# A hybrid state-space / attention / mixture-of-experts layer: copies of Q and K through outside memory, and two projections at other places of a shared bank's order

## What is computed

```python
# three sub-layers; x is (8, 512, 128) float32, every step adds to the residual stream
def _L0_attn_a_ref(x, W_in, Kx, Kz, W_xproj, W_dt, b_dt, A_log, D, W_out):     # state-space layer
    h = jnp.einsum('bld,ed->ble', x, W_in)
    xb, zb = jnp.split(h, 2, axis=-1)
    xb = _dwconv_silu(xb, Kx)
    zb = _dwconv_silu(zb, Kz)
    proj = jnp.einsum('blc,oc->blo', xb, W_xproj)
    dt_raw, b_raw, c_raw = proj[..., :8], proj[..., 8:16], proj[..., 16:]
    delta = jnp.clip(jax.nn.softplus(jnp.einsum('blr,cr->blc', dt_raw, W_dt) + b_dt), 0.0001, 1.0)
    b_term, c_term = jnp.tanh(b_raw), jnp.tanh(c_raw)
    a = jax.nn.softplus(A_log) + 0.0001
    decay = jnp.clip(jnp.exp(-delta[..., None] * a), 0.0001, 1.0)
    drive = (1.0 - decay) * (b_term[:, :, None, :] * xb[..., None])
    # scan over time: state = decay*state + drive;  y = sum(state*c) + D*xb
    return jnp.einsum('bld,ed->ble', jnp.concatenate([y, zb], axis=-1), W_out)

def _L0_attn_b_ref(hidden_states, Wq, bq, Wk, bk, Wv, bv, Wo, bo):             # attention, 16 heads of 8
    q, k, v = proj(hidden_states, Wq, bq) * scaling, proj(..., Wk, bk), proj(..., Wv, bv)
    scores = jnp.einsum('bhsd,bhtd->bhst', q, k) + chunk_attention_mask(S)     # chunks of 10, 25 to the left
    out = jnp.einsum('bhst,bhtd->bhsd', jax.nn.softmax(scores, axis=-1), v)
    return jnp.einsum('bse,fe->bsf', out, Wo) + bo

def _L0_ffn_ref(x, w_router, w_gating, w_gate, w_up, w_down):                  # 8 experts, all of them
    g = jnp.einsum('bsh,ehf->ebsf', x, w_gate)
    u = jnp.einsum('bsh,ehf->ebsf', x, w_up)
    expert_out = jnp.einsum('ebsf,efh->ebsh', jax.nn.silu(g) * u, w_down)
    return jnp.einsum('ebsh,bse->bsh', expert_out, cw)                         # cw: routing weights

x = x + _L0_attn_a_ref(_layernorm(x), ...)
x = x + _L0_ffn_ref(_layernorm(x), ...)
x = x + _L0_attn_b_ref(_layernorm(x), ...)
x = x + _L0_ffn_ref(_layernorm(x), ...)
```

## Time and profile before

| what | us |
|---|---|
| three runs: lowest, median, highest | 1697.87, 1698.93, 1699.07 |
| the profiled execution, its own time | 1692.36 |
| its span (first to last instruction) | 1690.5 |
| outside the span | 1.86 |

### The profile page before, as it was taken

How to read it: one execution, slowest core, us unless ns; L and a number is a source line. 1 busy time by engine, 2 the same in 40 slices (tenths; PEclk the granted TensorE clock), 3 DMA queues, 4 the chain that set the end, 5 groups by cost and what they waited for, 6 DMA issues and landing times. The chain is left out here.

```text
span 1690.5 us, 31436 instructions
## 1 busy us (share of the span) xinstructions
PE 1560.0 (92%) x12484; PEld 1305.2 (77%) x12484; DVE 1025.8 (61%) x2316; ACT 949.1 (56%) x1302; POOL 410.8 (24%) x403
## 2 busy tenths in 40 slices
PE   5389978999999899998999999989999999999998
PEld 2278866888778787787878778777788888888887
DVE  5556656765766567666665576556755675476543
ACT  5273737753686456836666486356743665276421
POOL 5332331422213222124211241113411221022000
PEclk9999989999999999999999999999999999999999
DMA  5010110002000200010001200021001000100000
GB/s 180 13 38 26 60 55 10 34 10 57 2 22 31 58 12 2 29 53 34 8 1 36 77 3 8 1 74 41 1 1 51 7 1 2 51 2 8 1 7 7
DMA packets 39426, 47.11 MB, mean 28 GB/s; under 512 B 5120, under 2 KB 21504, under 8 KB 39280
## 3 DMA queue, kind: packets, MB, share of 16 engines
q1 hardware_dynamic: 39280, 45.10, 8.7%
HBM read 25.97 MB, written 2.33 MB: 17 GB/s over the span
## 5 line engine op out<-in xcount | busy, mean ns | idle before, releaser
L948 ACT ACTIVATE h<-pg 128x512 f32<-128x512 f32 x512 | 304.5, 598 | 609.5 <-PE pg L261 607.0
L892 PE MATMUL pd<-w_down,h 128*128 128x128 f32 x4096 | 544.3, 282 | 0.6 <-DVE x L974 0.6
L892 PEld LDWEIGHTS pd<-w_down,h 128*128 128x128 f32 x4096 | 511.3, 195 | 31.5 <-issue 9.0
L994 DVE TENSOR_TENSOR h<-h,pu 128x512 f32<-128x512 f32 x512 | 347.2, 680 | 187.4 <-PE pu L261 185.9
L799 POOL TENSOR_TENSOR att_arena<-att_arena 100x500 f32<-100x500 f32 (+2 forms) x192 | 172.9, 900 | 613.5 <-DVE att_arena L741 605.8
L259 PE MATMUL pg<-ffn_x_hi,w_gate_hi 128*128 128x512 f32 x512 | 247.7, 484 | 0.0
L259 PE MATMUL pu<-ffn_x_hi,w_up_hi 128*128 128x512 f32 x512 | 205.7, 402 | 9.5 <-DVE h L994 9.5
L260 PE MATMUL pg<-ffn_x_lo,w_gate_hi 128*128 128x512 f32 x512 | 205.6, 402 | 0.0
L261 PE MATMUL pg<-ffn_x_hi,w_gate_lo 128*128 128x512 f32 x512 | 205.1, 401 | 0.0
L260 PE MATMUL pu<-ffn_x_lo,w_up_hi 128*128 128x512 f32 x512 | 205.0, 400 | 0.0
L261 PE MATMUL pu<-ffn_x_hi,w_up_lo 128*128 128x512 f32 x512 | 204.7, 400 | 0.0
(11 more groups left out here) (170 smaller groups left out, 1778.5 us busy)
## 6 DMA issues: line engine op xcount, KB each, us to landing
arena<-bc_spread SPq DMA_DIRECT2D x56, 256.0 KB
q<-qk_parts SPq DMA_DIRECT2D x128, 64.0 KB, 2.1
k<-qk_parts SPq DMA_DIRECT2D x128, 64.0 KB, 2.1
arena<-in_x SPq DMA_DIRECT2D x8, 256.0 KB, 2.8
x<-in_x SPq DMA_DIRECT2D x8, 256.0 KB, 3.3
h<-in_w_gate SPq DMA_DIRECT2D x8, 256.0 KB, 6.5
h<-in_w_up SPq DMA_DIRECT2D x8, 256.0 KB, 2.8
w_down<-in_w_down SPq DMA_DIRECT2D x8, 256.0 KB, 4.3
```

Source lines behind the costliest of these rows:

```text
L892: last = nc.tensor.matmul(pd[:, t * P:(t + 1) * P], h_b[:, d % NH, t * P:(t + 1) * P], wd[:, d % NCH, :], start=d % CPE == 0 and t == 0, s ...
L948: nc.scalar.activation(h_b[:, c % NH, :], pg[c % 2][:, :], ACT.Silu).then_inc(gate_done, 1)
L994: nc.vector.tensor_tensor(h, h, pu[d % 2][:, :], ALU.mult).then_inc(h_done, 1)
```

## The change

Q and K go by way of two outside buffers, used in turn: four transfers of 256 KB write both parts of Q and K out whole, and eight of 256 KB bring them back, each into every fourth partition of `q3` or `k3` for all four groups at once. The transfer of a rounded part starts after ACT has written it, without waiting for DVE; the eight come behind all four. The C tile of batch 2, with slot 46, falls between them. For batches 3 to 7 W_in moves from o-5 to o-6.5 in the order of the shared bank, ahead of the transpose of the FFN's rows, and its convolution and silu move with it on DVE and ACT. For batches 2 to 7 the B and C projection moves from the middle of step o+1 to its end, half a chunk behind dt, and ACT's tanh (and the logarithm behind it) to the middle of the next step.

```diff
--- before.py
+++ after.py
@@ -50,7 +50,7 @@
     if i == 2:
         return dict(ln=30, win=32.5, dt=36, k=(40, 43, 46, 49), y=54.5)
     o = NCH * (2 * i - 4)
-    return dict(ln=o - 8, win=o - 5, dt=o + 1, k=(o + 7, o + 13, o + 26, o + 32), y=o + 42)
+    return dict(ln=o - 8, win=o - 6.5, dt=o + 1, k=(o + 7, o + 13, o + 26, o + 32), y=o + 42)
 
 
 T_SSM = [_ssm_slots(i) for i in range(B)]
@@ -130,6 +130,7 @@
         xb2, zb, delta, tot, cv, sxT = (arena[:, i, :] for i in range(6))
         btile, ctile = ([arena[:, i + s, :] for s in range(2)] for i in (6, 8))
         bc_t = sb("bc_rows", [2 * DSTATE, L])
+        qk_d = [nc.dram_tensor(f"qk_rows{s}", (2, 2, P, L), F32, kind="Internal").ap() for s in range(2)]
         bc_d = [nc.dram_tensor(f"bc_spread{s}", (2 * DSTATE, L), F32, kind="Internal").ap() for s in range(2)]
         x_raw = arena[:, 3, :].rearrange("p (t d) -> p t d", t=TT)
         dec = arena[:, 4:6, :]
@@ -196,6 +197,7 @@
         dec_clip = sem("dec_clip")
         y_part, y_done, b_moved, c_moved = sem("y_part"), sem("y_done"), [sem("b_moved0"), sem("b_moved1")], [sem("c_moved0"), sem("c_moved1")]
         x_hi, qk_hi, qk_moved = sem("x_hi"), sem("qk_hi"), sem("qk_moved")
+        qk_out = [[sem(f"{v}_{part}_out") for part in ("hi", "lo")] for v in "qk"]
         att_done = sem("att_done")
         s_max, s_sub, s_exp, x2_bias = sem("s_max"), sem("s_sub"), sem("s_exp"), sem("x2_bias")
         act_step, dve_step, pool_step = sem("act_step"), sem("dve_step"), sem("pool_step")
@@ -379,6 +381,8 @@
                 for v in range(2):
                     last = nc.tensor.matmul(ps[:, :], wdt[v][:, :], xs, start=v == 0, stop=v == 1)
                 b.fill(last, ("dt", i))
+                if i >= 2:
+                    yield at["dt"] + 0.5
                 ps = b.take(pe, ("bc", i))
                 for v in range(2):
                     last = nc.tensor.matmul(ps[0:2 * DSTATE, :], wbc[v][:, :], xs, start=v == 0, stop=v == 1)
@@ -423,6 +427,8 @@
                 yield at["dt"] + 0.5
                 b.wait_free(act, ("dt", i))
                 link.count(nc.scalar.activation(delta, delta, ACT.Exp))
+                if i >= 2:
+                    yield at["dt"] + 1
                 b.wait(act, ("bc", i))
                 b.free(nc.scalar.activation(bc_t[:, :], b.ps(("bc", i))[0:2 * DSTATE, :], ACT.Tanh,
                                             scale=pk("bc_sign")[0:2 * DSTATE, :]), ("bc", i))
@@ -618,7 +624,7 @@
                         ab.fill(last, name)
 
                 yield at(1 / 6)
-                pe.wait_ge(qk_moved, 16 * 32 * (j + 1))
+                pe.wait_ge(qk_moved, 16 * 8 * (j + 1))
                 scores(0)
                 for n in range(NUNIT):
                     i, p = UNITS[n]
@@ -721,7 +727,7 @@
                     nq, nk, _, m0 = size(i)
                     mask = pk("mask")[:, m0:m0 + nk]
                     if n == 0:
-                        dve.wait_ge(qk_moved, 16 * 32 * (j + 1))
+                        dve.wait_ge(qk_moved, 16 * 8 * (j + 1))
                     if n >= 2:
                         ab.wait(dve, ("t", j, n - 2, 1))
                     for rr in range(2):
@@ -771,14 +777,25 @@
             @staticmethod
             def sp(sp, link, j):
 
-                for w, (v, dst, parts) in enumerate((("q", q3, (0, 0, 1, 1)), ("k", k3, (0, 1, 0, 1)))):
-                    for g in range(4):
-                        yield T_ATT[j] + 7 + 2 * w + 0.5 * g
-                        if g == 0:
+
+                qk_r = qk_d[j % 2]
+                yield T_ATT[j] + 7
+                if j >= 2:
+                    sp.wait_ge(qk_moved, 16 * 8 * (j - 1))
+                for w, v in enumerate("qk"):
+                    for part in range(2):
+                        yield T_ATT[j] + 7 + 0.5 * w
+                        if part == 0:
+                            sp.wait_ge(qk_hi, 2 * j + w + 1)
+                        else:
                             ab.wait_free(sp, (v, j))
-                        for i, part in enumerate(parts):
-                            sp.dma_start(dst[i::4, g, 0:L].bitcast(F32),
-                                         qk_s[32 * g:32 * g + 32, w, part, :].bitcast(F32)).then_inc(qk_moved, 16)
+                        sp.dma_start(qk_r[w, part], qk_s[:, w, part, :].bitcast(F32)).then_inc(qk_out[w][part], 16)
+                yield T_ATT[j] + 8
+                for w, (dst, parts) in enumerate(((q3, (0, 0, 1, 1)), (k3, (0, 1, 0, 1)))):
+                    for i, part in enumerate(parts):
+                        sp.wait_ge(qk_out[w][part], 16 * (j + 1))
+                        sp.dma_start(dst[i::4, :, 0:L].bitcast(F32),
+                                     qk_r[w, part].rearrange("(g e) l -> e g l", g=4)).then_inc(qk_moved, 16)
 
             @staticmethod
             def pool(pool, link, j):
```

## The result

The changed kernel takes 1642.8 us (median; 1642.5 to 1643.2). Its time is 0.968 of the kernel's before, with a 95% interval of 0.9658 to 0.9703, or 50 to 58 us less than a median of 1698.4. The forecast was 1656 and its range 1634 to 1677. Of all runs in this document two, both of the kernel with only the B and C projection's slots moved, stand apart (1784 and 1940 us, at a granted clock of 0.845 and 0.755), and the ratios leave them out.

What follows compares the result with a forecast made beforehand. PE was taken as the bound, busy 1560 of 1690.5 us. Terms 22.4 + 10.4 + 0 + 9.9 + 4.0 - 4.0 = 42.7 us, off the 1698.9 us median, gave 1656 us; range 1634 to 1677.

Steps and rivals of the forecast that it cites:

- Copies, seven attentions: PE's waits for K before first scores vanish in seven attentions: 22.4 us, plus 10.4 us of granted clock.
- The path: Twelve 256 KB issues replace 32 of 64 KB; Q and K are there 13 us after the first issue.
- Attention 0: First attention gains 0 us (from -2 to +8.6): PE would stop at the up products for `h` behind the B tile.
- 64 KB of outs, then three times 128 KB from 198 on, 22 us at 20 GB/s, so 220: In attention 0, outs, C tile, copies in and B tile queue on the same two engines; B tile comes no sooner.
- the copies spread over all 16 engines, 192 KB for each: Twelve Q and K transfers give each of 16 engines 192 KB, taking 9.6 us.
- W_in's slot: W_in ahead of the FFN's transpose, batches 3 to 7: net 9.9 us gained, plus 4 us of clock.
- The B and C projection: Moved to its step's end: 5.6 us of bank waits removed, 9.6 us added by ACT; net -4.0 us (+5.6 to -15).
- the 9.6 of new waits: ACT's lateness after the projection's move costs a new wait of 1.6 us (0 to 3.5) in each of six batches.
- PE can give way by about one chunk: Behind ACT's later tanh and logarithm, PE has about one chunk of slack, 2.3 us less what table loads took.
- Sum: Whole kernel: 22.4 + 10.4 + 0 + 9.9 + 4.0 - 4.0 = 42.7 us gained, 1656 us against the median.
- Rivals A and B: A: all comes back, attention 0 too, 1629, chance 0.12. B: ACT late, 4.5 us per batch, 1676, chance 0.18.
- rival C: In attentions 2 and 4 the wait for K becomes one for `h` behind a B tile: 1671 us, chance 0.10.

## Why the prediction was right, and where not

**Copies, seven attentions (22.4 us and 10.4 of clock): right.** All seven waits are gone. The path was right too: 12 issues at 0.32 to 0.61 us, K there 11 to 14 us after the first (13 forecast). The experiment with 32 pieces on the way back shows that it is the issues. That the copies alone gave 32 us where these two terms have 32.8 is in part luck, since the 32 hold the loss at attention 0 too. Behind attention 0 the copies gave 35.7 us in the profiled execution: 29.5 without the stretch behind attention 5, against 32.8, and 6.2 in that stretch, for the late B tile of batch 7. The prediction looked for tiles among the copies in attentions 2 and 4 and has no term for this one.

**Attention 0 (0 us, from -2): a few us too good.** The mechanism was as I put it, PE stopping at the up products for an `h` that stands behind the B tile. The step that failed is its working, "64 KB of outs, then three times 128 KB from 198 on, 22 us at 20 GB/s, so 220". It started from two idle engines. They were not: four tiles had been issued from 180 on and one at 192.4, and the five landed at 187.2, 192.3, 198.0, 203.0 and 208.1, 5.0 to 5.6 us apart, so that the first transfer out stood behind the last of them and landed 12 us after its issue, and SP stood still for 6.3. The tile came at 227.2. Attention 0 lost 5.2 us by the traces (6.3 by the medians), held against the kernel that gives it back its old copies; my bound was a loss of 2.
That the copies spread over all 16 engines, 192 KB for each, was my estimate; the copies in had a share of 0.90. The tile's other form brings the share from 0.13 to 0.59, lands its 128 KB in 3.0 us and takes POOL's waits away.

**W_in's slot (9.9 us and 4): right.** Alone it gave 14 us. The wait for the convolution was 2.0 us (2.9 forecast) and ACT's copies cost 2.8 to 3.7 (3.3 forecast).

**The B and C projection (-4.0 us): wrong in sign.** It gave 3.6 us in the changed kernel and 5.8 with fast tiles; the 5.6 us for the bank were right, and of the 9.6 of new waits at most 2.4 exist, 1.5 before scores and 0.9 for ACT's copies. No run shows the 1.6 us a batch that the 9.6 are added up from: they were my estimate of what ACT's lateness leaves of the chunk by which PE can give way. ACT's timeline in batch 7, to be held against the earlier trace rows, shows the lateness:

```profile
1079.48 1.28 ACT L965 ACT_TABLE_LOAD   x1
1080.97 0.60 ACT L965 ACTIVATE h<-pg 128x512 f32<-128x512 f32 x1 [0.21 <-PE pg L263]
1081.46 0.67 ACT L433 ACTIVATE bc_rows<-side_ps,pack 16x512 f32<-16x512 f32 x1
1082.15 1.28 ACT L436 ACT_TABLE_LOAD   x1
```

The silu takes a load of 1.28 us behind exp, and tanh follows the silu with no load between (1080.97 and 1081.46). It is so in all six batches: one load more between exp and the logarithm, which starts 4.4 to 5.5 us after exp, where before it was 2.5 to 2.7. In the whole kernel ACT has 4 loads more (296 for 292), which are its 4 instructions more (1306 for 1302).
Then "PE can give way by about one chunk": DVE's idle time ahead of its clip did rise, from 16.4 to 29.0 us, but PE's waits for `h` in the two kernels with fast tiles are the same 3.5 us with and without the move. The lateness was there and was nearly all covered. I had given it a price from 0 and put 1.6 us on it without a row that showed PE coming that near.

**Sum.** Forecast 42.7, between the profiled executions 49.7. Four spans split it: before 1690.5, with the copies alone 1658.3, with W_in's slot as well 1644.8, changed 1640.8. So the copies gave 32.2 us, W_in's slot 13.5 and the B and C projection 4.0, where the prediction has 32.8, 13.9 and -4.0. The 7 us are the projection's 8, less 1. That the copies' term fits so well is owed to the loss at attention 0 and the gain at batch 7, neither of them forecast, which cancel to within 1 us. Against the medians the miss is 13 us (1656 for 1642.8), and the other 6 have a source of their own: the prediction took its terms from an execution 6.6 us faster than the median and subtracted them from the median, as if those 6.6 us would stay. They went too: the changed kernel's profiled execution and its median are 0.2 us apart. That they are lower clock behind PE's waits is argued from the spread of the runs (last section), not tried. Rivals A and B are both out: attention 0 doesn't come back, and ACT isn't the late one. What rival C feared for attentions 2 and 4 came in neither; PE's only long wait for `h` behind the copies is that of attention 0.

## What to carry to other kernels

Where a transfer is late, count issues first: a copy in cost the queue 0.6 us at 64 KB and at 256 KB. Before transfers are put on a queue, add up what is already on the engines that they use, for each engine and not for the mean of sixteen, and ask which transfer's landing the queue itself will wait for. A wait that is only postponed on an engine off the critical path needs a row that shows the other engine arriving before it is given a price. And a part's forecast that comes true in the sum is worth splitting by place: here a loss of 5.6 us and an unforeseen gain of 6.2 stood behind an agreement to 1 us.

## What the runs showed of the hardware that was not expected

A tile of the form [2, 64, 512] moves at 44 GB/s, and the same bytes as two transfers of [64, 512] land in 3.0 us. While whole tiles are outstanding, issuing stalls too: in the changed kernel one of four transfers out took 3.1 us to issue, where the median is 0.44, and the issue of one tile 7.2; with half tiles no transfer out took over 0.53 and no half tile over 1.6.

Runs differ with the clock that they are granted. The kernel before took 1688 to 1701 us in the runs of these groups, at a mean clock of 0.984 to 0.973, and its variants with 32 copies were spread over 7 to 15 us. The changed kernel's four runs lie within 0.7 us, those of the other kernels with short copies within 1 to 4. The kernels with W_in's slot alone and with the projection's alone had a granted clock of 0.975 and 0.974 in their profiled executions, against 0.981 for the one before, and took 6.8 and 10.1 us more in them than their medians. So where PE waits for 2 to 6 us at many places, a single execution can be off by 0.6%. That the waits make the spread is argued from these groups, not tried.
